# Second layer's cross-attention with its steps placed one by one (outputs three batches behind the scores), and the last block's context attention with exponentials read from PSUM

## The reference, cut to what matters

```python
x = x + tanh(g_xattn[1]) * L1_xattn(layernorm(x), ctx_512, Wq, Wk, Wv, Wo, bo)

def L1_xattn(q, kv, Wq, Wk, Wv, Wo, bo):
    qh, kh, vh = heads(q @ Wq), heads(kv @ Wk), heads(kv @ Wv)      # 16 heads of 64
    attn = softmax(einsum('bhnd,bhmd->bhnm', qh, kh) * 64 ** -0.5)
    return concat(einsum('bhnm,bhmd->bhnd', attn, vh)) @ Wo + bo
```

```python
xn, yn = layernorm(x) * lnx_g + lnx_b, layernorm(ee) * lny_g + lny_b      # ee = ctx_512
q, k, v = einsum('bsc,hcd->bhsd', xn, wq), einsum('btc,hcd->bhtd', yn, wk), ...
a = softmax(einsum('bhsd,bhtd->bhst', q, k) * 32 ** -0.5)                 # no mask here
x_out = x + concat(einsum('bhst,bhtd->bhsd', a, v)) @ li1_w + li1_b
```

## Time and profile before

| | |
|---|---|
| median of 3 runs | 5404.17 us (5402.6 to 5416.16) |
| profiled execution, its own time | 5395.1 us |
| its span, first to last instruction | 5393.3 us |
| mean granted clock of TensorE | 0.925 of full |
| PE busy over the span | 4696.6 us (87%) |
| DVE, ACT, POOL busy | 3795.1 us (70%), 2899.9 us (54%), 2176.5 us (40%) |

### The profile page before, as it was taken

One profiled execution on the slowest core, in us unless ns is written; L12 is line 12 of the kernel. 1 busy time (PEld: TensorE's weight loads), 2 busy tenths in 40 slices (PEclk: granted clock), 3 DMA queues, 4 the chain that ended last, 5 costly groups with the idle time before them and its releaser, 6 DMA issues. The chain is left out here.

```text
span 5393.3 us, 135149 instructions
## 1 busy us (share of the span) xinstructions
PE 4696.6 (87%) x42171; PEld 3414.4 (63%) x42171; DVE 3795.1 (70%) x9705; ACT 2899.9 (54%) x7246; POOL 2176.5 (40%) x3095
## 2 busy tenths in 40 slices
PE   7998998999952699688989988999988899998898
PEld 4665668888852466455556666666666677776554
DVE  6776867777766333577767768888877899997444
ACT  4665765555530233344455548888873555554354
POOL 5552001011127100566633338888878333333200
PEclk9998999999975899777799999999999999999888
DMA  1004200000011344100000000000000000000000
GB/s 41 7 10 189 89 1 6 5 5 5 5 57 43 110 138 136 46 21 21 29 11 1 0 6 1 0 0 0 0 7 1 3 2 2 2 2 7 0 14 18
DMA packets 108951, 140.36 MB, mean 26 GB/s; under 512 B 35832, under 2 KB 83256, under 8 KB 103996
## 3 DMA queue, kind: packets, MB, share of 16 engines
q1 hardware_dynamic: 100544, 120.88, 6.6%
q0 software_dynamic: 8192, 16.79, 1.0%
HBM read 47.44 MB, written 58.72 MB: 20 GB/s over the span
## 5 line engine op out<-in xcount | busy, mean ns | idle before, releaser
L285 ACT ACTIVATE l3a_probs<-l3a_scores,l3a_mx 128x128 f32<-128x128 f32 x1024 | 363.5, 402 | 0.4 <-issue 0.4
L2273 POOL TENSOR_TENSOR l3a_probs<-l3a_probs,l3a_later 128x512 f32<-128x512 f32 x256 | 325.8, 1273 | 82.9 <-ACT l3a_probs L285 82.1
L191 POOL TENSOR_TENSOR l1x_ve<-l1x_mv,eps 128x1 f32<-128x1 f32 x64 | 12.3, 192 | 648.8 <-DVE l1x_mv L183 648.8
L1757 POOL TENSOR_TENSOR l2f_hid<-l2f_prod,l2f_route 128x512 f32<-128x512 f32 x128 | 152.3, 1195 | 254.3 <-DVE l2f_prod L1904 244.4
L2321 PE MATMUL l3a_scores<-l3a_keys,l3a_qT 128*128 128x512 f32 x512 | 251.2, 600 | 3.6 <-POOL l3a_keys L2259 3.6
L285 ACT ACTIVATION_READ_ACCUMULATOR l3a_probs<-l3a_scores,l3a_mx 128x1 f32 x1024 | 248.1, 242 | 0.0
L2259 POOL TENSOR_TENSOR l3a_keys<-l3a_kT,head 128x2048 f32<-128x2048 f32 x64 | 230.5, 3602 | 2.9 <-ACT l3a_kT L2390 2.9
L1643 PE MATMUL l1e_h<-l1e_xhi,l1f_parts 128*128 128x512 f16 x640 | 204.2, 380 | 9.7 <-DVE l1e_gated L1701 8.2
L310 ACT ACTIVATE l3c_hiT<-l3c_turned 77x512 f16<-77x512 f32 x256 | 150.4, 588 | 106.7 <-PE l3c_po L331 104.2
L2259 POOL TENSOR_TENSOR l3c_keys<-l3c_kT,head 128x1232 f32<-128x1232 f32 x64 | 144.1, 2252 | 156.5 <-ACT l3c_kT L2390 156.5
L317 DVE SCALAR_TENSOR_TENSOR l1x_loT<-l1x_turned,l1x_hiT 77x512 f16<-77x512 f32 x256 | 168.9, 679 | 49.6 <-ACT l1x_hiT L310 49.5
(11 more groups left out here) (587 smaller groups left out, 17280.5 us busy)
## 6 DMA issues: line engine op xcount, KB each, us to landing
l_rows<-l0f_zeros SPq DMA_DIRECT2D x34, 1024.0 KB, 27.1
l1f_parts<-l1f_split SPq DMA_DIRECT2D x40, 512.0 KB, 3.6
l1e_x_in<-l_rows SPq DMA_DIRECT2D x40, 256.0 KB, 2.8
l1f_down<-l1f_w SPq DMA_DIRECT2D x40, 256.0 KB, 2.4
l_rows<-l1e_y_out SPq DMA_DIRECT2D x40, 256.0 KB, 2.7
l1f_w<-in_L_W SPq DMA_DIRECT2D x16, 256.0 KB, 3.6
out_x<-x_res SPq DMA_DIRECT2D x16, 256.0 KB, 2.0
x_res<-in_x SPq DMA_DIRECT2D x1, 3840.0 KB, 12.2
```

The costliest lines, as they stand in the source:

```text
L285: last = act.activation(self.probs[it.par][:, h, :], self.view(c)[:, h - a, :], ACT.Exp, bias=self.mx[it.par][:, h:h + 1], scale=-1.0, acc ...
L1757: pool.tensor_tensor(hid[k % 2][:, :].rearrange("p (e m) -> p e m", m=M), prod[k % 2][:, :].rearrange("p (e m) -> p e m", m=M), rt.w[it.pa ...
L2273: pool.tensor_tensor(v, v, later[:, :].unsqueeze(1).to_broadcast([P, 4, T]), ALU.mult).then_inc(s_masked, 1)
```

## The change: what it does, and the diff

In `l1_xattn` all five lists are rewritten with `placed`: PE runs `score0` 2 rounds behind, `turn_p` 3 and 4, `weigh` 3 and 4, `turn_o` 4 and 5 and `output` 5 (before: scores 2, `turn_p` and `weigh` 3 with `turn_p0` 2, outputs 4), in another order inside the round; the other engines follow. SP's context load is split: the two loads of `pair_ctx` wait only for the scores of two batches before, `ctx1` for the low half of the context of two batches before, on a semaphore of its own. In `l3_attention` the context stage gets `direct=True`: the four `shift` steps of DVE go, `fetch_q` scales by -scale, ACT runs 16 exponentials per batch from PSUM without `accum_out` in place of 4 from SBUF, a bank of scores is free after the exponential instead of after the shift, and all its lists are rewritten with `placed`. The row sums stay on DVE.

```diff
--- before.py
+++ after.py
@@ -275,15 +275,18 @@
...
         act.activation(v, v, ACT.Exp, scale=self.scale).then_inc(self.s_exp, 1)
-    def exponential_of_bank(self, act, it, c, total):
+    def exponential_of_bank(self, act, it, c, total=None):
         a, b = self.first[c], self.first[c + 1]
...
         for h in range(a, b):
-            last = act.activation(self.probs[it.par][:, h, :], self.view(c)[:, h - a, :], ACT.Exp,
-                                  bias=self.mx[it.par][:, h:h + 1], scale=-1.0, accum_out=total[it.par][:, h:h + 1])
+            dst, src, bias = self.probs[it.par][:, h, :], self.view(c)[:, h - a, :], self.mx[it.par][:, h:h + 1]
+            if total is None:
+                last = act.activation(dst, src, ACT.Exp, bias=bias, scale=-1.0)
+            else:
+                last = act.activation(dst, src, ACT.Exp, bias=bias, scale=-1.0, accum_out=total[it.par][:, h:h + 1])
         last.then_inc(self.s_exp, 1)
...
@@ -1948,6 +1951,7 @@
...
         sm = Softmax(st, g, scores, HELD, KEYS, scale, turned, split=True)
+        s_ctx1 = st.sem2("s_ctx1")
         s_ctx, s_set = st.sem2("s_ctx"), st.sem("s_set")
...
@@ -1962,12 +1966,12 @@
...
                         sp.wait_ge(sm.s_scores, due)
-                    if (due := nth(it, 4, ago=2)) is not None:
-                        sp.wait_ge(sm.s_values, due)
                     one = g.ctxT_d[:, bass.ds(it.b, 1), :].rearrange("c b t -> c (b t)")
...
                     sp.dma_start(pair_ctx[p][CTX:P, KEYS:2 * KEYS], one).then_inc(s_ctx[p], 16)
-                    sp.dma_start(ctx1[p][:, 0:CTX], g.ctx_d[:, bass.ds(it.b, 1), :].rearrange("t b c -> t (b c)")).then_inc(s_ctx[p], 16)
+                    if (due := nth(it, ago=2)) is not None:
+                        sp.wait_ge(s_clo, due)
+                    sp.dma_start(ctx1[p][:, 0:CTX], g.ctx_d[:, bass.ds(it.b, 1), :].rearrange("t b c -> t (b c)")).then_inc(s_ctx1[p], 16)
                 skewed(sp, g.B, [(context, 0)], 2)
...
@@ -1985,7 +1989,7 @@
...
                 pool.wait_ge(s_gated_bo, 1)
-                skewed(pool, g.B, [(add_bias, 2), (lambda it: ln.inverse_deviation(pool, it), 0)], 4)
+                skewed(pool, g.B, [(add_bias, 2), (lambda it: ln.inverse_deviation(pool, it), 1)], 8)
             @block.tensor
...
@@ -2020,7 +2024,7 @@
...
                 def score(it, c):
-                    pe.wait_ge(s_ctx[it.par], loads(it, 3))
+                    pe.wait_ge(s_ctx[it.par], loads(it, 2))
                     pe.wait_ge(s_qT, nth(it, 2))
...
@@ -2056,12 +2060,12 @@
...
                     last.then_inc(s_y, 1)
-                steps = {**numbered("turn_p", lambda it, c: sm.turn(pe, it, c), 4, 3), **numbered("score", score, 3, 2),
-                         **numbered("weigh", weigh, 4, 3), "turn": (turn, 1), **numbered("queries", queries, 2, 1),
-                         **numbered("turn_o", turn_o, 2, 4), "output": (output, 4)}
-                steps["turn_p0"] = (steps["turn_p0"][0], 2)
-                skewed(pe, g.B, in_order(steps, "turn_p1 turn_o0 score0 turn_p2 weigh0 turn_p3 turn score1 turn_o1 weigh1 queries0 "
-                                                "score2 weigh2 turn_p0 weigh3 output queries1"), 6)
+                steps = {**numbered("turn_p", lambda it, c: sm.turn(pe, it, c), 4), **numbered("score", score, 3),
+                         **numbered("weigh", weigh, 4), "turn": (turn, 1), **numbered("queries", queries, 2),
+                         **numbered("turn_o", turn_o, 2), "output": (output, 4)}
+                skewed(pe, g.B, placed(steps, "score1:3 score2:3 weigh1:4 turn_o1:5 turn_p3:4 queries1:2 turn_p0:3 weigh2:4 "
+                                              "output:5 turn:1 weigh3:4 score0:2 turn_p1:3 turn_p2:3 queries0:1 weigh0:3 "
+                                              "turn_o0:4"), 8)
             @block.scalar
...
@@ -2072,7 +2076,7 @@
...
                 def round_context(it):
-                    act.wait_ge(s_ctx[it.par], loads(it, 3))
+                    act.wait_ge(s_ctx1[it.par], loads(it))
                     if (due := nth(it, 4, ago=2)) is not None:
...
@@ -2089,12 +2093,12 @@
...
                     act.copy(oT[it.par][:, 4 * c:4 * c + 4, :].rearrange("p i t -> p (i t)"), py[:, :]).then_inc(s_oT, 1)
-                steps = {**numbered("fetch_p", lambda it, c: sm.fetch(act, it, c), 4, 3),
-                         **numbered("exp", lambda it, c: sm.exponential(act, it, c), 3, 2),
-                         **numbered("fetch_o", fetch_o, 2, 4), "context": (round_context, 1), "fetch_x": (lambda it: ln.fetch(act, it, s_q, 2), 1),
-                         **numbered("fetch_q", fetch_q, 2, 1)}
-                skewed(act, g.B, in_order(steps, "fetch_p0 fetch_p1 fetch_o0 fetch_p2 fetch_x exp0 fetch_p3 fetch_o1 fetch_q0 exp1 "
-                                                 "exp2 fetch_q1 context"), 6)
+                steps = {**numbered("fetch_p", lambda it, c: sm.fetch(act, it, c), 4),
+                         **numbered("exp", lambda it, c: sm.exponential(act, it, c), 3),
+                         **numbered("fetch_o", fetch_o, 2), "context": (round_context, 1), "fetch_x": (lambda it: ln.fetch(act, it, s_q, 2), 1),
+                         **numbered("fetch_q", fetch_q, 2)}
+                skewed(act, g.B, placed(steps, "fetch_o0:5 fetch_q0:2 exp0:3 context:3 fetch_o1:5 fetch_p3:4 fetch_q1:2 "
+                                               "fetch_p0:3 exp1:3 fetch_x:1 fetch_p1:3 exp2:3 fetch_p2:3"), 8)
             @block.vector
...
@@ -2126,14 +2130,14 @@
...
                     dve.scalar_tensor_tensor(x, y_p, g.gates[:, 1:2], x, ALU.mult, ALU.add).then_inc(s_x, 1)
-                steps = {**numbered("maximum", lambda it, c: sm.maximum(dve, it, c), 3, 2),
-                         **numbered("shift", lambda it, c: sm.shift(dve, it, c), 3, 2), **numbered("divide", divide, 4, 3),
+                steps = {**numbered("maximum", lambda it, c: sm.maximum(dve, it, c), 3),
+                         **numbered("shift", lambda it, c: sm.shift(dve, it, c), 3), **numbered("divide", divide, 4),
                          "statistics": (lambda it: ln.statistics(dve, it), 0), "normalize": (lambda it: ln.normalize(dve, it), 1),
-                         **numbered("remainder", lambda it, c: sm.remainder(dve, it, c), 4, 3),
+                         **numbered("remainder", lambda it, c: sm.remainder(dve, it, c), 4),
                          "context": (context_remainder, 2), "add": (add, 4)}
-                later(steps, "divide3")
-                skewed(dve, g.B, in_order(steps, "normalize divide3 remainder0 remainder1 maximum0 divide0 shift0 remainder2 maximum1 context divide1 "
-                                                 "remainder3 divide2 maximum2 statistics shift1 shift2 add"), 6)
+                skewed(dve, g.B, placed(steps, "shift0:4 remainder1:5 normalize:2 divide0:5 maximum1:4 remainder2:5 divide1:5 "
+                                               "maximum2:4 shift1:4 remainder3:5 divide2:5 statistics:0 shift2:4 remainder0:4 "
+                                               "add:6 context:4 divide3:5 maximum0:3"), 8)
 class Norm:
@@ -2215,7 +2219,7 @@
...
         pa, po = st.ps("pa"), st.ps("po")
-        sm = Softmax(st, g, scores, [4] * 4, T, scale, turned, split=True, direct=first)
+        sm = Softmax(st, g, scores, [4] * 4, T, scale, turned, split=True, direct=True)
         n3 = Norm(st, g, "n3", P, P)
...
@@ -2279,8 +2283,8 @@
...
                     steps.update(deviation_y=(lambda it: ny.inverse_deviation(pool, it), 2), begin_y=(begin_y, 4))
-                    names = "deviation_y spread deviation3 begin_y"
-                skewed(pool, g.B, (placed if first else in_order)(steps, names), 8)
+                    names = ("spread:3 begin_y:5 deviation_y:1 deviation3:0")
+                skewed(pool, g.B, placed(steps, names), 8)
             @block.tensor
...
@@ -2317,7 +2321,7 @@
...
                     if (due := nth(it, 4, c, back=4)) is not None:
-                        pe.wait_ge(sm.s_exp if first else sm.s_shift, due)
+                        pe.wait_ge(sm.s_exp, due)
                     pe.matmul(scores[c][:, 0:G4 * T], qT[it.par][:, c, :], keys[it.par][:, c, :, :].rearrange("p h t -> p (h t)"),
...
@@ -2354,9 +2358,9 @@
...
                 else:
-                    names = ("turn_p0 score0 turn_p1 turn score1 turn_o queries output turn_p2 score2 weigh0 turn_p3 keys "
-                             "weigh1 score3 weigh2 values weigh3")
-                skewed(pe, g.B, (placed if first else in_order)(steps, names), 8)
+                    names = ("values:2 weigh2:4 weigh3:4 turn_p0:3 turn_p1:3 score0:2 turn_o:4 turn:1 score1:2 score2:2 queries:1 "
+                             "output:4 turn_p2:3 keys:1 weigh0:3 weigh1:3 turn_p3:3 score3:2")
+                skewed(pe, g.B, placed(steps, names), 8)
             @block.scalar
...
@@ -2378,10 +2382,7 @@
...
```

(21 more changed lines are left out.)

## The result

The changed kernel takes 5228.56 us (median of 4 runs, 5203.98 to 5231.24) against 5403.39 for the kernel before beside it: ratio 0.9664, 95% interval 0.9642 to 0.9685. The direction was right, and the size was not. The two profiled executions lie 167 us apart (5395.1 and 5228.24), the medians 175.

What follows compares the result with a forecast made beforehand. It took PE to nearly bound both stages, with its idle time to be won: -70 (l1x order) - 42 (l3c order) + 5 (l1x ends) = -107 us, giving 5297 us from 5404.2; range 5274 to 5352 for 8 in 10 runs.

Steps and rivals of the forecast that it cites:

- the two hand-overs: PE's waits: l1x's weigh for DVE to empty po (0.59 us), l3c's turn for DVE's values remainder (0.66 us).
- PE's idle time: What can be won without taking work from PE: 0.91 us a batch in l1x, 0.71 in l3c.
- the term was -42: l3c, new order: turn's stall of 0.66 us goes in each of 64 batches, -42 us.
- l1x, the middle: New order removes both stalls of PE: 10.45 us a batch, 1.09 less, over 64 batches -70 us.
- sum of steps: l1x's bound for the largest gain: PE's step times added, 10.2 us a batch, giving -86 us.
- The ends of l1x: Outputs come a round later; the further round costs between 0 and 11.5 us, taken as +5.
- SP: 0 forecast: l1x: pair_ctx queues behind ctx1's later wait, but nothing on PE waits for it; cost 0.
- DVE and ACT in l3c: DVE falls to 8.3 us a batch, ACT rises to 8.4; both stay under PE's 10.5.
- Half of the waits stays: Rival, both stages: new lists still meet a wait of some 0.4 us per batch; -54 us, 5350; chance 0.20.
- `hat` meets `spread`: Rival, l3c: DVE's normalisation slows beside POOL's spread, 0.333 to 0.58-1.51 us; gain lost, 5339; chance 0.05.
- ACT as the bound: Rival, l3c: exponentials of 0.468 us make ACT take 12.1 us a batch; 5395, no change; chance 0.05.
- The loop in l1x: Rival: a loop of waits through all engines sets l1x's pace, 13.0 us a batch; slower, 5464; chance 0.03.

Runs made afterwards that it cites:

- e3: Kernel before with l3c's exponentials straight from PSUM and the shifts gone, but old lists and lags; 5415.71 us, ratio 1.0005.
- e6: Changed kernel with SP's old wait ahead of the pair_ctx loads in l1x; 5451.84 us, ratio 1.0197 to the kernel before.
- e8: Kernel before with only SP's split in l1x: pair_ctx loaded early, context semaphore of its own; 5339.3 us, ratio 0.9974.
- e4: Kernel before with l3c's new lists and lags, but DVE's shift kept right behind each maximum; 5483.55 us, ratio 1.0129.
- e11: Kernel before with l3c's new lists and depth, DVE's shifts kept but placed later than their maxima; 5371.56 us, ratio 1.0048.
- e10: Changed kernel with l3c's row sums taken by ACT in its exponentials and DVE's four sums gone; 5160.4 us, ratio 0.9662 to the kernel before.
- e5: Kernel before with PE's output moved ahead of the third weigh in l1x; 5467.3 us, ratio 1.0235.
- e9: Changed kernel with PE's values right ahead of turn_o in l3c; 5303.74 us, ratio 0.9925 to the kernel before.
- e12: Changed kernel with l3c's values late on PE and ACT's and DVE's parts of it moved back too; 5337.86 us, ratio 0.9886 to the kernel before.

## Why the prediction was wrong in size

The chain of reasons held: the two hand-overs were what the diff takes away, and nothing of their size took their place. Both middles became PE's, but for the 0.22 us at `weigh1`. The size failed in one way throughout.

**The failed step: PE's idle time was taken as the most that could be won.** The prediction put it as "what can be won without taking work from PE is its idle time", and for l3c as "0.71 x 64 = -45" at best. Measured: 1.20 us a batch (11.29 to 10.09), which over 64 batches is the stage's 77 us where the term was -42. PE's recorded busy time per batch fell from 599.41/640 x 11.29 = 10.57 to 576.42/580 x 10.09 = 10.03 us with the same matmuls at the same clock. The busy time of before held waits. A group of matmuls is drawn to its modelled end, some 0.16 us beyond the point where the next one may start: a `turn_p` of 0.60 us is followed after 0.44 where nothing is awaited. This row of the kernel before stands ahead of the `turn` of the earlier trace rows:

```profile
4506.88 0.60 PE L299 MATMUL l3c_turned<-ident,l3c_probs 128*77 128x128 f32 x4
```

From it to `turn` at 4508.14 are 1.26 us, so 1.26 - 0.44 = 0.82 were lost where the bracket says 0.66. A wait shorter than 0.16 us has no bracket at all: `output` of l3c stands behind `queries` in both kernels, and its second matmul starts 183 ns after its first before (the median) and 112 ns after the change. Worked out from the starts of all of PE's matmuls in the two middles, us a batch before and after, scaled to the batch:

| step | l3c | l1x |
|---|---|---|
| turn_p | 2.74, 1.92 | 3.05, 1.74 |
| score | 2.34, 2.23 | 2.23, 2.17 |
| queries | 0.95, 0.93 | 1.87, 1.78 |
| output | 0.97, 0.89 | 1.87, 1.88 |
| weigh | 1.52, 1.45 | 1.47, 1.47 |
| turn_o, turn | 0.71, 0.62 | 1.06, 1.04 |
| keys, values | 2.07, 2.05 | none |

In l3c 0.82 of the 1.20 us went at `turn` and 0.38 in small pieces at the banks of scores, `output`, `weigh` and `turn_o`; e3 shows by itself that such pieces come and go without the idle time following. That each of them was a wait is likely, but not shown one by one.

**l1x, the middle: -70 forecast, -93 measured** ((11.54 - 10.08) x 64). There starts were read, not idle time, which is why the miss is smaller: only two stalls were taken out of one batch of 11.33, which left 10.46. The other two `turn_p` (0.49 and 0.47 us instead of 0.44) and one of `queries` (0.97 instead of 0.89) held small waits too. And the batch shown was one of the short ones: the view of the earlier trace rows has a second wait, which stands in half of the batches,

```profile
PE l1x_py L2049 <- DVE l1x_o L2113: 19.5, 26, 0.8
```

so that the `turn_p` ahead of `turn_o0` takes 1.05 us in the mean and not the 0.75 of that batch. Even the bound "sum of steps", 10.2, was too high, because the 0.47 us of its `turn_p` was not a free one (0.44 here).

**The ends of l1x: +5 forecast.** The whole stage is 100.8 us shorter and the middle's share is 93, so the ends gave 7 rather than cost 5. The extra round did not show as a price; the last 20 us ran at a granted clock of 0.92 instead of 0.75, so nothing was "wholly at half speed". (The upper bound of 11.5 us would not have covered that: PE fills 10.09 us of a batch at 1.00, so one wholly at half the clock takes up to some 20, an estimate.)

**SP: 0 forecast, right, but for the split as a whole the wrong question.** By e6 it is worth nearly 300 us at the new depth and by e8 7 us at the old one.

**DVE and ACT in l3c.** An exponential was forecast at 0.24 us and ACT at 8.4 us a batch; 0.24 and 485.39/57.5 = 8.44 came. "What shows it right" named 0.34 us of duration; 0.32 was shown. That fewer microseconds of DVE are worth nothing by themselves, e3 bears out; that they are what lets the order be kept, e4 and e11 do.

**The rivals.** Half of the waits stays: no, PE's recorded idle time is under 0.07 us a batch, and with what is hidden it is 0.2 at most. `hat` meets `spread`: no, 333 ns at the median and 346 at most, and none of the 64 runs beside a `spread`. In the kernel before one of the 64 did (at 4202.26 us, `spread` from 4200.41 to 4202.66), and it is the one of 487 ns in the earlier trace rows. That single case agrees with the rule of the Trainium skill ("SBUF — State Buffer", "Who interferes with whom"); the changed kernel doesn't put it to the test. ACT as the bound: no, it carries 9.4 us in e10 without harm. The loop in l1x: no, though e6 shows a loop of another kind, through SP and a DMA, which I had dismissed in one sentence. (Its sum was off a little as well: 13.0 us a batch against 11.54 is +93, not +97.)

Of the miss of 68 us, 23 lie in l1x's middle, 12 in its ends and 35 in l3c; these make 70, and the other stages and rounding the rest.

## What to carry to other kernels

Where one engine is nearly full, bound a gain by the starts of its steps against the shortest start-to-start distance of the same step anywhere in the trace, and not by recorded idle time. Before deepening a ring, look at what the in-order DMA queue waits for: a load behind a late release turns a saving into a loss, and moving the releasing instruction does so too. A new order and the relief of a second engine can each be worth nothing or less alone and be worth much together, so try them together as well.

## What the runs showed of the hardware

A stall in e11 could cost four times its length: behind a wait of 1 us at `weigh` stood matmuls at 1.2 GHz, in a batch of 13.8 us instead of 9.9, while the same recorded idle time of 0.66 us at the same place in another batch was followed by no fall. In e6 and e5, where PE waited for loads, the granted clock of the middle was 0.88 and 0.93. Yet in e9 and e12, where PE's recorded busy time is lower than in e11 (437 and 442 of 500 us against 476), the granted clock stayed 1.00. What tells these cases apart stays open. The changed kernel's gain in l3c did not depend on it, since both middles ran at 1.00 before and after.
